# Spare matrix products in TensorE's waits across four stages, and a last normalisation ahead of VectorE's free steps

## What is computed

```python
x = x + _L1_xattn_ref(_layernorm(x), ctx, ctx, mask, ...)   # L1x: 16 heads of width 8, 512 keys
x = x + _L1_ffn_ref(_layernorm(x), ...)                     # L1f, then moe
x = x + _L2_xattn_ref(_layernorm(x), ctx, ...)              # L2x: 16 heads of width 64, 512 keys
...
# inside _L1_ffn_ref
x = x + _layernorm(_attention(x, ...), ln1_g, ln1_b)        # 16 heads of width 8, 256 keys
x = x + _layernorm(_moe(x, ...), ln2_g, ln2_b)
# _moe: 8 experts, all computed, 128 -> 512 -> 128, exact gelu
for e in range(E):
    h = gelu(xt @ W1[e] + b1[e]) @ W2[e] + b2[e]
    out = out + combine[:, e:e + 1] * h
```

## Time and profile before

| | us |
|---|---|
| median of three executions | 573.88 (573.83 to 576.77) |
| profiled execution, its own time | 577.15 |
| its span, first to last instruction | 575.3 |
| mean granted clock of TensorE over the span | 0.963 |
| TensorE busy | 522.9 |
| VectorE busy | 436.3 |
| ScalarE busy | 340.7 |

### The profile page before, as it was taken

One profiled execution on the slowest core, in us unless ns is written; L12 is line 12 of the kernel. 1 busy time (PEld: TensorE's weight loads), 2 busy tenths in 40 slices (PEclk: granted clock), 3 DMA queues, 4 the chain that ended last, 5 costly groups with the idle time before them and its releaser, 6 DMA issues.

```text
span 575.3 us, 12996 instructions
## 1 busy us (share of the span) xinstructions
PE 522.9 (91%) x4775; PEld 299.6 (52%) x4775; DVE 436.3 (76%) x1235; ACT 340.7 (59%) x679; POOL 231.5 (40%) x228
## 2 busy tenths in 40 slices
PE   8989999999889899978995889959999999999996
PEld 4346666667743233333333567714556655864564
DVE  6999999997376889836676689876777777578763
ACT  3578888888235366644662748637777778621302
POOL 2037777777314600000000526513777777700100
PEclk9989999999999999998799879968999999999999
DMA  9770000001220000000000213000000000000000
GB/s 243 131 224 3 2 2 3 1 2 38 68 80 0 2 1 3 1 1 2 1 1 19 74 38 88 5 2 1 1 2 2 2 1 3 1 1 1 1 1 19
DMA packets 24082, 15.40 MB, mean 27 GB/s; under 512 B 8083, under 2 KB 22230, under 8 KB 23894
## 3 DMA queue, kind: packets, MB, share of 16 engines
q1 hardware_dynamic: 24022, 14.60, 9.6%
HBM read 14.33 MB, written 0.26 MB: 25 GB/s over the span
## 4 chain that ended last, share of the span: by engine, by line
PE 50%; issue 22%; DVE 13%; POOL 7%; ACT 6%; DVEq 0%; POOLq 0%; ACTq 0%
PE pspair L477 7%; PE psM L439 6%; PE psS L463 4%; PE psO L492 4%; PE pspair L892 3%; PE pspair L654 3%; PE psO L679 2%; PE pspair L463 2%; ACT PP L1224 2%; POOL PP L2270 2%; POOL PP L2267 1%; DVE Oall L1830 1%; PE pspair L402 1%; PE psS L402 1%; PE psS L880 1%
## 5 line engine op out<-in xcount | busy, mean ns | idle before, releaser
L2258 POOL TENSOR_TENSOR ln_rs<-ln_ve,minus_half 128x4 f32<-128x4 f32 x10 | 10.2, 1021 | 192.0 <-DVE ln_ve L1481 188.9
L477 PE MATMUL pspair<-ident,PP 128*128 128x128 f32 x512 | 83.0, 286 | 2.7 <-ACT PP L1224 2.5
L477 PEld LDWEIGHTS pspair<-ident,PP 128*128 128x128 f32 x512 | 55.2, 143 | 30.3 <-issue 19.1
L492 PE MATMUL psO<-V,PP 128*128 128x64 f16 x1536 | 65.7, 193 | 2.1 <-DVE Oall L1624 2.0
L1590 DVE TENSOR_TENSOR PP<-pspair,PP 128x512 f16<-128x512 f32 x64 | 44.0, 688 | 30.1 <-ACT PP L1208 30.1
L1288 ACT ACTIVATE PP<-pspair 128x1024 f32<-128x1024 f32 x48 | 46.5, 1021 | 30.9 <-PE pspair L665 30.9
L492 PEld LDWEIGHTS psO<-V,PP 128*128 128x128 f16 x1536 | 61.5, 98 | 5.9 <-DVE PP L1590 2.8
L2267 POOL TENSOR_TENSOR PP<-acc,one 128x512 f16<-128x512 f32 x32 | 33.3, 1040 | 65.7 <-ACT acc L1206 65.7
L1224 ACT ACTIVATE PP<-scores_m,nm 128x512 f32<-128x512 f32 x64 | 46.6, 728 | 4.6 <-DVE nm L1574 4.6
L2267 POOL TENSOR_TENSOR PP<-y_sb,one 128x512 f16<-128x512 f32 x32 | 33.3, 1040 | 19.8 <-ACT y_sb L1206 19.8
L2270 POOL TENSOR_TENSOR PP<-y_sb,PP 128x512 f16<-128x512 f32 x32 | 37.1, 1159 | 2.5
(11 more groups left out here) (537 smaller groups left out, 1239.0 us busy)
## 6 DMA issues: line engine op xcount, KB each, us to landing
W<-in_L_ffn_W SPq DMA_DIRECT2D x16, 256.0 KB, 2.9
bigw<-in_L_xattn_w_q SPq DMA_DIRECT2D x2, 512.0 KB, 6.9
bigw<-in_L_xattn_w_kv SPq DMA_DIRECT2D x1, 1024.0 KB, 4.7
V<-in_ctx SPq DMA_DIRECT2D x1, 512.0 KB, 3.8
bigw<-in_L_xattn_w_v SPq DMA_DIRECT2D x1, 512.0 KB, 5.1
mask_b<-in_mask_BxS_ff SPq DMA_DIRECT2D x1, 512.0 KB, 6.9
bigw<-in_L_xattn_w_k SPq DMA_DIRECT2D x1, 512.0 KB, 6.1
bigw<-in_L_xattn_w_o SPq DMA_DIRECT2D x1, 512.0 KB, 4.0
```

What stands on the lines that cost most here:

```text
L477: mm = pe.transpose(bank[f"T{j % 2}"][:, k * P:(k + 1) * P], Pb[j % 4][:, k * P:(k + 1) * P], ident[:])
L492: mm = pe.matmul(bank["O"][:, (j % UPH) * a.dv:(j % UPH + 1) * a.dv], (PTH, PTL)[ppart][j % 4][:, k * P:(k + 1) * P], (VH, VL)[vpart][:, b ...
```

## The change

Two things are done. Spare products are put in at 15 places of the code of TensorE's stream, 96 products in all when it runs, more where some stood already: at the end and (L1F) at the start of the packed attentions, ahead of the layer norm's turn behind L1f, in the expert stage, at the start of L2x, and three places of L3f. A helper `ring_spare` puts them into the ring's next bank, so they wait until that bank has been read. `packed` on VectorE gets a second list `behind`, whose steps come after the last `norm`; three of L1F's four free steps move there.

```diff
--- before.py
+++ after.py
@@ -580,6 +580,10 @@
             k = turn_of[a.name] = turn_of.get(a.name, -1) + 1
             return take(pe, name, turns[k % 3]), full[turns[k % 3]]
 
+        def ring_spare(pe, a, n):
+
+            spare(pe, turns[(turn_of[a.name] + 1) % 3], n)
+
         def selector(s, g):
 
             return RSEL[:, s, HG * g:HG * g + HG, :].rearrange("p j x -> p (j x)")
@@ -632,7 +636,7 @@
                 if nr < a.lead and a.mask and part == 0:
                     pe_fill_value(pe, 6 + nr, ("S3", "T0", "T1")[nr])
                 elif nr < a.lead:
-                    for _ in range(2 if a.mask else 1):
+                    for _ in range(2):
                         pe.matmul(pairs[0][:, 0, :], ident16[:], ident16[:].unsqueeze(1).broadcast_to([P, 4, P]),
                                   start=True, stop=True)
 
@@ -698,7 +702,7 @@
                 repeat_k(pe, 0, 0, take(pe, f"{n}.RK0.0", "S3"), full["S3"])
             if a.mask:
                 pe_fill_value(pe, 5, "T1")
-            spare(pe, "S0", 1 if a.mask else 3)
+            spare(pe, "S0", 1 if a.mask else 4)
             pe.wait_ge(free["S2"], fills["S2"])
             for r in range(-a.lead, a.rounds + 2):
                 if r == 0:
@@ -712,6 +716,8 @@
                 if r == 1:
                     for v in last_v:
                         emptied(pe, v)
+                if r + a.lead >= a.rounds and r <= a.rounds:
+                    ring_spare(pe, a, 4 if r == a.rounds else 2)
                 if 1 <= r <= a.rounds:
                     values(r - 1)
                 if (r + 1) % rpi == 0 and 0 <= (r + 1) // rpi < NG * B:
@@ -727,6 +733,8 @@
                             repeat_k(pe, g, c, ps, done)
                 g, q = divmod(r - 1, B * rpi)
                 if q == 0 and 1 <= g <= NG:
+                    if g == NG:
+                        ring_spare(pe, a, 3)
                     turn_out(g - 1)
                 if r + a.lead < a.rounds:
                     natural(r + a.lead, 1)
@@ -855,9 +863,9 @@
             pe_tiles(pe, "L1f.v", "S1", lambda t: XT[1][:, t * P:(t + 1) * P], lambda t: sq[:, 6, :], D)
             pe_packed(pe, L1F, ["L1f.v"])
             pe_out(pe, L1F, lambda c: sq[:, 7, :], 1)
+            spare(pe, "S0", 16)
+            pe_ln(pe, "L1g", XN[0])
             spare(pe, "S0", 3)
-            pe_ln(pe, "L1g", XN[0])
-            spare(pe, "S0", 2)
             emptied(pe, "L1g.xt")
             pe.wait_ge(sem("ld.moe"), 2 * 16)
             pe_tiles(pe, "L1f.gate", "M", lambda t: XT[0][:, t * P:(t + 1) * P], lambda t: gate_w[:], E)
@@ -898,14 +906,18 @@
                 for k2 in range(2):
                     if not (last and k2 == 1):
                         hidden(i, k2 + 1)
+                    else:
+                        spare(pe, "M", 4)
                     outputs(i, k2)
 
             pe.wait_ge(sem("moe.x"), 1)
             hidden(0, 0)
             hidden(0, 1)
+            spare(pe, "M", 5)
             outputs(0, 0)
             hidden(0, 2)
             pe_onehot_turn(pe, "moe")
+            spare(pe, "O", 10)
             pe_onehot_rows(pe, "moe", b2w)
             outputs(0, 1)
             with pe.Fori(1, E // 2 - 1) as i:
@@ -916,8 +928,11 @@
             pe_wide_values(pe, "L2", range(13, 2 * NC))
             pe.wait_ge(sem("L2.vsplit"), len(FILL))
             pe_first_keys(pe, L2X, ctxT, "ld.L2")
+            spare(pe, "O", 20)
             pe_ln(pe, "L2x", XN[1])
+            spare(pe, "O", 3)
             pe_first_query(pe, L2X, XT[1])
+            spare(pe, "O", 6)
             pe_attention(pe, L2X, ctxT, XT[1], [f"L2.V{v}" for v in range(2 * NC)],
                          lambda c: bigw[:, 3, c * P:(c + 1) * P], "ld.L2wo")
 
@@ -1058,6 +1073,8 @@
             spare(pe, "T0", 2)
             scores3(1)
             for g in range(2):
+                if g == 0:
+                    spare(pe, "T0", 3)
                 pe.wait_ge(sem("L3f.exp"), g + 1)
                 b = ("S0", "S3")[g]
                 ps = take(pe, f"L3f.pt{g}", b)
@@ -1089,6 +1106,7 @@
 
             ps = take(pe, "L3f.oT", "O")
             pe.matmul(ps[:, 0:GS], o3p[:], twice[:], start=True, stop=True).then_inc(full["O"], 1)
+            spare(pe, "T0", 1)
             emptied(pe, "L3f.oT")
             ps = take(pe, "L3f.o2", "O")
             pe.matmul(ps[0:GS, 0:D], o3T[:], l3wo[:], start=True, stop=True).then_inc(full["O"], 1)
@@ -1675,7 +1694,7 @@
                 recip(*group)
                 norm(*group)
 
-            def packed(a, last=()):
+            def packed(a, last=(), behind=()):
                 n, rpi, kt = a.name, a.rpi, a.kt
 
                 def stat(nr, k):
@@ -1734,6 +1753,9 @@
                     g, q = divmod(r - 1, B * rpi)
                     if q == 0 and 1 <= g <= NG:
                         norm(g - 1)
+                    if r == a.rounds + 1:
+                        for step in behind:
+                            step()
                     if nr < a.rounds:
                         stat(nr, 2)
                         stat(nr, 3)
@@ -1849,9 +1871,10 @@
                 dve.tensor_tensor(Vaug[:, 0:NT, :, 0:DN], ps[:].rearrange("p (t h d) -> p t h d", t=NT, d=DN),
                                   wide(rowp["L1_ffn_bv"]).rearrange("p t (h d) -> p t h d", d=DN), ALU.add)\
                     .then_inc(free_of("L1f.v"), 1)
-                packed(L1F, [lambda: split_W1(0, 0), lambda: split_W1(0, 1),
-                             lambda: link(dve.tensor_tensor(XN[1][:], XN[1][:], wide(rowp["L1_ffn_ln1_b"]), ALU.add)),
-                             l3_positions])
+                packed(L1F, [lambda: split_W1(0, 0)],
+                       [lambda: split_W1(0, 1),
+                        lambda: link(dve.tensor_tensor(XN[1][:], XN[1][:], wide(rowp["L1_ffn_ln1_b"]), ALU.add)),
+                        l3_positions])
                 ps = filled(dve, "L1f.y")
                 dve.tensor_tensor(y_sb[:], ps[:].rearrange("p (t d) -> p t d", t=NT), wide(rowp["L1_ffn_bo"]),
                                   ALU.add).then_inc(free_of("L1f.y"), 1)
```

## The result

The changed kernel takes 571.82 us (median of 22 executions, 569.8 to 574.81); the kernel before took 575.16 beside it (22 executions, 571.56 to 578.61). The ratio is 0.9949, with an interval of 0.9933 to 0.9966: faster by 0.5%, 3.3 us, where 566.5 was predicted. The profiled execution of the changed kernel took 571.43 us, with a span of 569.7 and a mean clock of 0.994 against 0.963.

A forecast was written before the change was run, and what follows sets the result against it. TensorE, close to busy through four half-clock stretches of 37.5 us together, was taken to put the clock on the path. Terms -3.8 +0.5 +0.7 -0.9 -1.1 -1.0 -0.9 -3.5 sum to -10.0: 577.15 to 567.1, stated 566.5, range 562.5 to 571.0.

The forecast's parts named there:

- the term for the start of L1F: Start of L1F's attention: five more spares keep the clock full through the half-clock stretch at 270.3 to 280.5; -3.8 us.
- the -3.0 of the expert stage: Turn, gate, first experts -1.1, bias rows -1.0, loop -0.9, from full clock behind L1f.
- the signs that the prediction named: Clock 9 from slice 4, L1F rounds 3.8 apart, turn waits under 0.6, bias product 1.0, outputs 2.84, norm behind turn.
- The gap rule: Rival: only idle gaps between matmul bursts drop the clock, so L1F's stretch stays; -6.2 in all, 570.9 us; chance 0.13.
- Spares eat the gain: Rival: thin margins overshoot by 3 us in all and one stretch stays slow; 572 to 573 us; chance 0.08.
- Packed ends: Ends of the two packed attentions: spares overshoot their waits, +0.5 us in L1X and +0.7 in L1F.
- The norm: VectorE's last norm in L1F begins earlier with its free steps behind it; -0.9 us.
- Turn, gate, bias rows and loop: From L1f's turn through the experts: full clock gives -1.1 to the gelus, -1.0 at the bias rows, -0.9 in the loop.
- the experts pass on little: Rival: VectorE or ScalarE takes over at once, the expert stage's -3.0 shrinks to about 0.5; 569.6 us; chance 0.12.
- Start of L2x: Spares fill the waits at L2x's start; turn, queries, keys and scores run at full clock; -3.5 us.
- L3f: Five spares, 1.1 us in all, go into waits on ScalarE and VectorE; 0, bounds 0 and +1.1.
- The base: Start of the sum: profiled 577.15 against median 573.88; a half-clock stretch, about that at 335.2, seemed missing from the median's executions.

The follow-up runs named there:

- lead_alone: Kernel before with only the five more spares at the start of L1F's attention; ratio 0.9995 to the kernel before.
- quiet_no_lead: best_two with the five spares at the start of L1F taken out again; median 566.65 us.
- best_two: best plus four spares: three between the gate and the first experts' products, one in L3f; 566.22 us, ratio 0.9826 to the kernel before.
- no_ring: Changed kernel without the 24 ring spares at the ends of L1X and L1F; 570.75 us, ratio 0.9944 to the kernel before.
- before: The kernel before, unchanged, in the profiled execution that the prediction read; 577.15 us.
- trim: Changed kernel without ring spares and without new spares around L1f's turn or in the experts; 570.38 us, ratio 0.9897 to the kernel before.
- before_second: The kernel before run again unchanged, for a second trace; 574.06 us over 12 executions, ratio 0.9988.
- norm_alone: Kernel before with only VectorE's last norm of L1F moved ahead of three free steps, no spares added; ratio 1.0005.
- l2x_alone: Kernel before with only the 29 spares at the start of L2x; 572.34 us, ratio 0.9984 to the kernel before.
- no_expert_spares: Changed kernel without the new spares around L1f's turn and in the expert stage; 571.77 us, ratio 0.9939 to the kernel before.
- early_fill: Changed kernel without ring spares, with 17 more spares in L0x and L0f; 566.98 us, ratio 0.9839 to the kernel before.
- best: early_fill with GpSimd's two additions into the residual moved to VectorE; 565.99 us, ratio 0.9851 to the kernel before.
- dve_adds: Changed kernel with GpSimd's two additions into the residual moved to VectorE; 572.08 us, ratio 0.9948 to the kernel before.

## Why the prediction was wrong

Two steps failed, each by more than 2.5 us: the term for the start of L1F, **-3.8**, which is about -1.0 in the mean, and the -3.0 of the expert stage, which is about -0.4. Behind both stands that the sum was made on one execution. With them right, the sum would have been -4.6 instead of -10.0.

At L1F the mechanism is borne out as far as traces show it: the clock fell there in three of five traces without the five spares and in none of nine with them. Whether they hold it by their full width or only as more work no run tells apart. In the pair of profiles L1f went from 56.20 to 52.57, -3.63 against the -4.0 of -3.8 +0.7 -0.9. But the term was read from an execution in which a 10.2 us stretch stood there. In the five traces without these spares it was 10.2 us once, 3.4 twice and absent twice; against the same kernel without a fall L1f paid 3.85, 1.3, 1.2, 0 and 0, a mean of 1.3, and the spares cost 0.26 always. Five traces are few. The totals say the same with less precision: the spares gave 0.3 us by lead_alone's ratio and 0.4 between the medians of quiet_no_lead and best_two.

Most of the signs that the prediction named came true in the profile after: no stretch at half clock in L1F or at L2x, the waits ahead of both turns under 0.6 us, the outputs behind the bias rows at 2.85. They tell that the clock was held and not what that is worth. Only the clock at 9 from slice 4 on failed, by the stretch in L0f.

- **The gap rule** lost as a rule: the clock fell at L1F in three of five traces with no wait above 0.6 us in the 12 us before it, and with the same waits before it in the two where it did not fall; longer waits are not what made the difference. Its 570.9 came within 1 us of the time, by luck.
- **Spares eat the gain**, 572 to 573, lay nearest to 571.82, but not by its mechanism: the overshoot is 1.9 us, not 3, and its trace has no slow stretch where spares were put.
- **Packed ends**, +0.5 and +0.7: measured +0.77 and +0.85 (no_ring). The mechanism was right, the sizes a little small.
- **The norm**, -0.9: -0.89.
- **Turn, gate, bias rows and loop**, -1.1 -1.0 -0.9: in the pair of profiles -1.58. Counted from the stage's start, which is itself 1.10 earlier, the gelus come 1.38 earlier (forecast 1.1), but ohT behind VectorE's low parts only 0.27. The bias product gives 0.91 more (forecast 1.0), the loop 0.40 (forecast 0.9). So what failed here is the overlap: I had counted VectorE's idle time and not that it gets slower beside GpSimd as soon as the gelus come earlier. Over the executions it is less still. The bias rows and the loop were costed from a stretch of 6.8 us that stands in two of the seven traces without these spares (before 62.67, trim 62.62); the other five (before_second, norm_alone, lead_alone, l2x_alone, no_expert_spares) take 60.88 to 61.41. The mean is 61.5, against 61.1 with the spares. The rival "the experts pass on little" came true in this.
- **Start of L2x**, -3.5: -2.9, in every trace. The first scores come 2.05 us earlier after the norm, where the turn's 0.3 and the projections' 2.05 had made 2.35; the rest gave 0.9 where I had taken 1.2. One reading was loose: this stretch begins at 379.5, inside the wait of 4.61 (376.9 to 381.5) and not behind it.
- **L3f**, 0: its stages agree within 0.1 between the two profiles.
- **The base.** I weighed 577.15 against 573.88 and took the stretch at 335 for the missing one. In the traces that have no new spares there, falls came and went at five places, in L0x, L0f, L1x, L1f and at the bias rows. The changed kernel's profile had one in L0f that the profile before lacked, +1.70, though nothing was changed there.

The terms as the runs show them, -1.0 -0.4 -2.9 -0.9 +0.8 +0.9, make -3.5 us. Measured between the medians: -3.3. The first two are means of few traces, so part of this agreement is luck.

## What to carry to other kernels

Before costing a stretch at half clock, look whether other executions have it: a second trace, and the mean clock of every execution, tell a stretch that always comes (here at L2x, in four traces of four, and at the turn, in seven of seven) from one that comes at times. Then ask whether it is on the path: the one at L2x cost 2.9 us, the one at the turn next to nothing (an expert stage of 60.98 with it and 61.09 without). A wait filled with spare products is worth what the next engine lets through; look for what that engine will run beside once it starts earlier. Where a kernel's time scatters in steps with its mean clock, filling the places that fall can narrow the spread as well as lower the median, as it did in early_fill and best, though one execution of best_two still fell out.

## What I had not expected of the hardware

The same program, in the same place, kept its clock in one execution and lost it in another: before and before_second ran the same instructions from 263 to 270 us, and one fell. The Trainium skill, page TensorE: Matmul & The Clock Gate, section What's actually happening, says that the window in which activity is judged runs freely and is not reset when a kernel starts. These two traces agree with that, but do not show that it is the cause. And a place with no wait can fall: in dve_adds the clock went at 545.2, in L3f, with no idle time of TensorE above 0.15 us since 538.4, behind products of 2, 32 and 10 columns and a few wider ones, and the last stage was 6.1 us longer for it. The other thirteen traces have the same products there, two of them with one spare more, and no fall.
